# Routed expert slots: rows turned by DMA transposes of 16-bit planes instead of TensorE transposes, with eight row buffers

## The reference, cut to what matters

```python
xn = (x - mean(x)) / sqrt(var(x) + 1e-5)              # rows of 512
chosen = argmax(einsum('bsh,eh->bse', xn, gate_w))    # one of 8 experts
out = x + xn + xn @ expert_w[chosen].T                # 512 x 512 each
```

## Time and profile before

| | |
|---|---|
| median of 3 runs | 1007.43 us (1007.35 to 1007.58) |
| the profiled execution | 1007.09 us |
| its span, first to last instruction | 1005.3 us |
| PE busy | 966.4 us, 96% of the span |
| DVE busy | 674.9 us, 67% |
| ACT busy | 408.1 us, 41% |
| POOL busy | 402.1 us, 40% |
| mean granted TensorE clock | 0.989 of full speed |

### The profile page before, as it was taken

One profiled execution on the slowest core, in us unless ns is written; L12 is line 12 of the kernel. 1 busy time (PEld: TensorE's weight loads), 2 busy tenths in 40 slices (PEclk: granted clock), 3 DMA queues, 4 the chain that ended last, 5 costly groups with the idle time before them and its releaser, 6 DMA issues. The chain is left out here.

```text
span 1005.3 us, 16387 instructions
## 1 busy us (share of the span) xinstructions
PE 966.4 (96%) x5009; PEld 792.6 (79%) x5010; DVE 674.9 (67%) x1655; ACT 408.1 (41%) x704; POOL 402.1 (40%) x522
## 2 busy tenths in 40 slices
PE   7999999999999999999999999999857999999995
PEld 6788888888888888888888888888646888888884
DVE  6677777777777777777777687776985444444442
ACT  5333333333333333333333332332546666666662
POOL 1041616345261634626163362615273333333332
PEclk9999999999999999999999999999979999999998
DMA  9051022121302212130221203112265555555441
GB/s 322 12 178 43 22 105 79 48 86 42 126 32 95 83 44 88 40 126 33 95 84 43 97 31 126 41 44 85 84 220 178 159 160 166 168 159 161 138 149 55
DMA packets 47324, 101.70 MB, mean 101 GB/s; under 512 B 5781, under 2 KB 6549, under 8 KB 47264
## 3 DMA queue, kind: packets, MB, share of 16 engines
q1 hardware_dynamic: 33680, 61.93, 19.1%
q0 software_dynamic: 10800, 33.70, 8.7%
q10 hardware_dynamic: 2784, 5.31, 1.6%
HBM read 64.85 MB, written 37.90 MB: 102 GB/s over the span
## 5 line engine op out<-in xcount | busy, mean ns | idle before, releaser
L412 POOL TENSOR_TENSOR y_biased<-y_biased,gate 128x512 f32<-128x512 f32 x60 | 91.3, 1521 | 144.4 <-DVE y_biased L764 144.4
L481 POOL DMA_INDIRECT out<-gate,ids x71 | 69.9, 984 | 153.9 <-DVE gate L1029 115.2
L1355 PE MATMUL y<-expert_hi,x1T_hi 128*128 x284 | 119.3, 420 | 3.9 <-DVE x1T_lo L1023 3.9
L1029 DVE TENSOR_TENSOR gate<-y,x_rows 128x512 f32<-128x512 f32 x71 | 49.1, 691 | 108.2 <-PE y L1355 108.2
L1355 PE MATMUL y<-expert_hi,x1T_lo 128*128 x284 | 112.7, 397 | 0.0
L1355 PE MATMUL y<-expert_lo,x1T_hi 128*128 x284 | 112.3, 395 | 0.0
L1065 PE MATMUL gates<-GwT_hi,xT_hi 128*128 128x512 f32 x256 | 104.8, 409 | 0.0
L1065 PE MATMUL y<-DwT_hi,xT_hi 128*128 128x512 f32 x256 | 101.9, 398 | 0.5 <-DVE gateT L696 0.5
L1066 PE MATMUL gates<-GwT_lo,xT_hi 128*128 128x512 f32 x256 | 100.8, 394 | 0.0
L1067 PE MATMUL gates<-GwT_hi,xT_lo 128*128 128x512 f32 x256 | 100.3, 392 | 0.0
L1067 PE MATMUL y<-DwT_hi,xT_lo 128*128 128x512 f32 x256 | 100.3, 392 | 0.0
(11 more groups left out here) (246 smaller groups left out, 2372.8 us busy)
## 6 DMA issues: line engine op xcount, KB each, us to landing
x_rows<-routed_rows SPq DMA_DIRECT2D x71, 258.0 KB, 2.6
x_in<-L_attn_x SPq DMA_DIRECT2D x32, 512.0 KB, 4.4
x_rows<-L_attn_x SPq DMA_DIRECT2D x32, 512.0 KB, 4.4
raw_weights<-L_ffn_expert_w ACTq DMA_DIRECT2D x5, 1024.0 KB, 7.3
raw_weights<-L_ffn_expert_w SPq DMA_DIRECT2D x3, 1024.0 KB, 8.9
routed_rows<-padrow SPq DMA_DIRECT2D x9, 258.0 KB
out<-gate,ids POOLq DMA_INDIRECT x71, 2.8
raw_weights<-L_attn_D_w SPq DMA_DIRECT2D x1, 1024.0 KB, 8.1
```

Of the source, the lines that this page charges most:

```text
L412: nc.gpsimd.tensor_tensor(yb[:, i, :], yb[:, i, :], gate[:, i, :], ALU.mult).then_inc(S_["gated"], 1)
L481: nc.gpsimd.indirect_dma_start(out=out_rows, out_offset=bass.IndirectOffsetOnAxis(ap=ids[m][:, 0:1], axis=0), in_=res[m], in_offset=None, ...
L1029: nc.vector.tensor_tensor(res[m], Y[m % 2][:], rows[m][:, 0:D], ALU.add).then_inc(S_["slot_result"], 1)
L1355: ins = nc.tensor.matmul(Y[m % 2][:], x2T[a][:, k, m % 2 * P:(m % 2 + 1) * P], flat[w][:, bass.ds(first + k * D, D)], start=(k == 0 and a ...
```

## The change

`slot_turn` is gone from TensorE. In its place:

1. VectorE splits the normalised row of float32 into two planes of 16-bit halves: all first halves, then all second halves (`slot_split`), 1024 elements of 16 bits a partition.
2. SP issues one DMA transpose of this 128 x 1024 tile of 16-bit elements into another tile of SBUF (`flip`). It takes space in raw_weights that the expert matrices no longer need.
3. VectorE joins the planes again into float32 (`slot_merge`), into a single SBUF tile, `merged`. `slot_hi` and `slot_lo` read that tile where they read a PSUM bank before.

There are two buffers each for the halves and the turned planes, and one each for `rnorm` and `merged` (before, `rnorm` had four). The row buffers become eight (`M`), with R = 4 result buffers. The DVE order becomes merge(s + 1), sum(s - 1), lo(s + 1), split(s + 3), and ACT's hi(s + 1), norm(s + 3), base(s + 3). SP issues `load_slot(n)` and then `flip(n - 4)`. The wait for the last scattered rows, ahead of the loop of slots 48 and up before, now stands ahead of the load of slot 4, so ahead of the first flip as well.

```diff
-    M = 4
+    M, R = 8, 4
@@
-        rows = [xrow[0][:, m, :] for m in range(M)]
-        rnorm = [yb[:, m, :] for m in range(M)]
-        res = [gate[:, m, :] for m in range(M)]
+        rows = [xrow[m // NT][:, m % NT, :] for m in range(M)]
+        res = [gate[:, r, :] for r in range(R)]
+        rnorm, merged = yb[:, 0, :], yb[:, NT - 1, :]
+        halves = [yb[:, 1 + q, :].bitcast(u16) for q in range(2)]
+        flipped = [raw[:, 2, q, :].bitcast(u16).rearrange("p (k t) -> p k t", t=P) for q in range(2)]
@@ sync
+            def flip(s, q):
+
+                counted_waits(sp, (S_["slot_halves"], s + 1), (S_["slot_merged"], s - 1))
+                sp.dma_start_transpose(flipped[q], halves[q]).then_inc(slot_flip[q], 16)
+
+            AHEAD = 4
+            for m in range(AHEAD):
                 load_slot(m, m)
...
+            sp.wait_ge(rows_sent[1], 16 * NT * (NBLK // 2))
+            for m in range(AHEAD, M):
+                load_slot(m, m)
+                flip(m - AHEAD, m % 2)
             with sp.Fori(1, EARLY) as u:
                 for m in range(M):
                     load_slot(u * M + m, m)
-
-            sp.wait_ge(rows_sent[1], 16 * NT * (NBLK // 2))
+                    flip(u * M + m - AHEAD, m % 2)
@@ scalar
             def slot_hi(s, q):
-                act.wait_ge(S_["slot_turned"], s + 1)
+                act.wait_ge(S_["slot_merged"], s + 1)
                 wait(act, S_["slot_psum"], s - 1)
-                nc.scalar.activation(x2T[0][:, :, q * P:(q + 1) * P], by_block((TP, SC)[q]), ACT.Copy).then_inc(S_["slot_hi"], 1)
+                nc.scalar.activation(x2T[0][:, :, q * P:(q + 1) * P], by_block(merged), ACT.Copy).then_inc(S_["slot_hi"], 1)
...
-                wait(act, S_["slot_turned"], s - M + 1)
-                nc.scalar.activation(rnorm[m], rows[m][:, 0:D], ACT.Identity, bias=rows[m][:, SHIFT:SHIFT + 1],
+                wait(act, S_["slot_halves"], s)
+                nc.scalar.activation(rnorm, rows[m][:, 0:D], ACT.Identity, bias=rows[m][:, SHIFT:SHIFT + 1],
...
             def slot(s, m, turn):
 
-                slot_hi(s, m % 2)
-                if not (isinstance(s, int) and s == SLOTS - 1):
-                    slot_norm(s + 1, (m + 1) % M, turn + (m + 1) // M)
-                    slot_base(s + 1, (m + 1) % M)
+                if not (isinstance(s, int) and s + 1 >= SLOTS):
+                    slot_hi(s + 1, (m + 1) % 2)
+                if not (isinstance(s, int) and s + 3 >= SLOTS):
+                    enter(s + 3, (m + 3) % M, turn + (m + 3) // M)
@@ vector
+            def slot_split(s, q, pair):
+
+                dve.wait_ge(S_["slot_norm"], s + 1)
+                wait(dve, slot_flip[q], 16 * pair)
+                nc.vector.tensor_copy(halves[q].rearrange("p (h d) -> p h d", h=2),
+                                      rnorm.bitcast(u16).rearrange("p (d h) -> p h d", h=2)).then_inc(S_["slot_halves"], 1)
+
+            def slot_merge(s, q, pair):
+                counted_waits(dve, (slot_flip[q], 16 * (pair + 1)), (S_["slot_lo"], s))
+                nc.vector.tensor_copy(merged.bitcast(u16).rearrange("p (t h) -> p h t", h=2),
+                                      flipped[q].rearrange("p (h k) t -> p h (k t)", h=2)).then_inc(S_["slot_merged"], 1)
+
             def slot_lo(s, q):
                 dve.wait_ge(S_["slot_hi"], s + 1)
                 hi, lo = [h[:, :, q * P:(q + 1) * P] for h in x2T]
-                nc.vector.tensor_tensor(lo, by_block((TP, SC)[q]), hi.bitcast(f32), ALU.subtract).then_inc(S_["slot_lo"], 1)
+                nc.vector.tensor_tensor(lo, by_block(merged), hi.bitcast(f32), ALU.subtract).then_inc(S_["slot_lo"], 1)
...
             def slot(s, m, turn):
 
-                slot_lo(s, m % 2)
+                last = s if isinstance(s, int) else 0
+                if last + 1 < SLOTS:
+                    slot_merge(s + 1, (m + 1) % 2, turn * (M // 2) + (m + 1) // 2)
                 if not (isinstance(s, int) and s == 0):
                     slot_sum(s - 1, (m - 1) % M, turn - (m == 0))
+                if last + 1 < SLOTS:
+                    slot_lo(s + 1, (m + 1) % 2)
+                if last + 3 < SLOTS:
+                    slot_split(s + 3, (m + 3) % 2, turn * (M // 2) + (m + 3) // 2)
@@ tensor
-            def slot_turn(s, m):
-                bank = (TP, SC)[m % 2]
-                pe.wait_ge(S_["slot_norm"], s + 1)
-                wait(pe, S_["slot_lo"], s - 1)
-                for k in range(KD):
-                    ins = nc.tensor.transpose(bank[:, k * P:(k + 1) * P], rnorm[m][:, k * P:(k + 1) * P], ident[:])
-                ins.then_inc(S_["slot_turned"], 1)
```

More of the change, by code:

```diff
@@ L7, in preln_ssm_moe_kernel @@
                          gate_w, expert_w, out):
-    f32, f32r, bf16, i32 = mybir.dt.float32, mybir.dt.float32r, mybir.dt.bfloat16, mybir.dt.int32
+    f32, f32r, bf16 = mybir.dt.float32, mybir.dt.float32r, mybir.dt.bfloat16
+    i32, u16 = mybir.dt.int32, mybir.dt.uint16
     ALU, ACT, AX = mybir.AluOpType, mybir.ActivationFunctionType, mybir.AxisListType
@@ L112, in preln_ssm_moe_kernel @@
         dest = [kb(f"dest{q}", [P, NT], i32) for q in range(2)]
-        ids = [kb(f"ids{m}", [P, 1], i32) for m in range(M)]
+        ids = [kb(f"ids{r}", [P, 1], i32) for r in range(R)]
         count, tiles_f, cum, gap = kb("list_count", [1, E]), kb("list_tiles", [1, E]), kb("tiles_upto", [1, E]), kb("list_gap", [1, E])
@@ L178, in preln_ssm_moe_kernel @@
         row_loaded = [sem(f"row_loaded{m}") for m in range(M)]
-        out_sent = [sem(f"out_sent{m}") for m in range(M)]
+        out_sent = [sem(f"out_sent{r}") for r in range(R)]
+        slot_flip = [sem("slot_flip_even"), sem("slot_flip_odd")]
         def counted_waits(eng, *waits):
@@ L189, in by_block @@
         def by_block(bank):
-            return bank[:].rearrange("p (k t) -> p k t", k=KD)
+            return (bank if isinstance(bank, bass.AP) else bank[:]).rearrange("p (k t) -> p k t", k=KD)
         def state_tile(h, i):
@@ L365, in _ @@
                     load_slot(u * M + m, m)
+                    flip(u * M + m - AHEAD, m % 2)
             for s in range(FULL * M, SLOTS):
                 load_slot(s, s % M)
+                flip(s - AHEAD, s % 2)
+            for s in range(SLOTS - AHEAD, SLOTS):
+                flip(s, s % 2)
         @block.gpsimd
@@ L488, in slot @@
                 if not (isinstance(s, int) and s == 0):
-                    slot_store(s - 1, (m - 1) % M)
+                    slot_store(s - 1, (m - 1) % R)
             for m in range(M):
@@ L497, in _ @@
                 slot(s, s % M, FULL)
-            slot_store(SLOTS - 1, (SLOTS - 1) % M)
-            for m in range(M):
-                pool.wait_ge(out_sent[m], 16 * len(range(m, SLOTS, M)))
+            slot_store(SLOTS - 1, (SLOTS - 1) % R)
+            for r in range(R):
+                pool.wait_ge(out_sent[r], 16 * len(range(r, SLOTS, R)))
         @block.scalar
@@ L642, in slot_base, with enter @@
                                      scale=rows[m][:, GAIN:GAIN + 1]).then_inc(S_["slot_base"], 1)
+            def enter(s, m, turn):
+                slot_norm(s, m, turn)
+                slot_base(s, m)
             def slot(s, m, turn):
-                slot_hi(s, m % 2)
-                if not (isinstance(s, int) and s == SLOTS - 1):
-                    slot_norm(s + 1, (m + 1) % M, turn + (m + 1) // M)
-                    slot_base(s + 1, (m + 1) % M)
-            slot_norm(0, 0, 0)
-            slot_base(0, 0)
-            slot(0, 0, 0)
+                if not (isinstance(s, int) and s + 1 >= SLOTS):
+                    slot_hi(s + 1, (m + 1) % 2)
+                if not (isinstance(s, int) and s + 3 >= SLOTS):
+                    enter(s + 3, (m + 3) % M, turn + (m + 3) // M)
+            enter(0, 0, 0)
             experts(E_STEPS[5], NE)
-            for s in range(1, M):
+            enter(1, 1, 0)
+            enter(2, 2, 0)
+            slot_hi(0, 0)
+            for s in range(M):
                 slot(s, s, 0)
@@ L1052, in _ @@
                     slot_rows(FIRST, SLOTS - FIRST)
-            with dve.Fori(2, FULL) as u:
+            with dve.Fori(1, FULL) as u:
                 for m in range(M):
@@ L1357, in slot_product @@
                 ins.then_inc(S_["slot_psum"], 1)
-            def slot(s, m):
-                slot_turn(s, m)
-                if not (isinstance(s, int) and s == 0):
-                    slot_product(s - 1, (m - 1) % M)
             pe.wait_ge(S_["run_ready"], NBLK)
-            slot(0, 0)
             experts(E_STEPS[5], NE)
-            slot_turn(1, 1)
             pe.wait_ge(S_["expert_lo"], dve_count(NE))
@@ L1371, in _ @@
             pe.wait_ge(S_["expert_table"], 1)
-            slot_product(0, 0)
-            for m in range(2, M):
-                slot(m, m)
+            for s in range(M):
+                slot_product(s, s)
             with pe.Fori(1, EARLY) as u:
                 for m in range(M):
-                    slot(u * M + m, m)
```

(6 more changed lines are left out.)

29 lines of the change are left out of this document (17 added, 12 removed).

## The result

Four runs of the changed kernel gave a median of 1041.51 us (1040.9 to 1045.59), four of the kernel before 1007.5 on the same chip. The ratio is 1.0344, with a 95% interval from 1.0317 to 1.0372: 34 us slower, and 4.5 us above the 1037 us that were forecast.

A forecast was written before the change was run, and what follows sets the result against it. TensorE, busy 96% of the span, was taken to bound the kernel; after the change, full DMA engines at 3.6 us a slot. A 5.9 us later start plus 70 periods less 227.6 gave +30 on 1007.1: 1037 us, range 988 to 1190.

The forecast's parts named there:

- 70 P - 221.7: Change in total time: start 5.9 us later plus 70 slot periods, less 227.6 us; +30 us forecast.
- P: Slot period, from one TensorE product's start to the next: 3.6 us forecast; no change in time at 3.17.
- The copies: VectorE's split and merge, 1024 16-bit elements each: 0.70 us apiece, from the nearest float32 copies within SBUF.
- The rival of one element a cycle: VectorE's split and merge copies take 1.23 us each, period 4.0 us, 1065 us in all; chance 0.09.
- The ring D: Cycle of merge, hi, norm and split across VectorE and ScalarE, each releasing the next: 2.93 us a slot.
- The transpose's work: Time one DMA transpose takes of the 16 DMA engines: 1024 pieces at 31 ns, 2.0 us.
- The other end: Upper bound for the transpose: each of 1024 pieces costs a load packet's 0.109 us, 7.0 us of the engines.
- like the load: Rival: transposes take 0.98 us of the engines and land in 2.6; period 2.93 us, 990 us; chance 0.20.
- (D + L) / 2: Slot period set by latency, as a transpose has one iteration between split and merge: 3.4 us forecast.
- full engines: DMA engines' work a slot: load 0.98, store 0.63, transpose 2.0, together 3.6 us, taken as the period.
- L: Latency from the end of VectorE's split to the DMA transpose's turned data: 3.8 us forecast.
- The clock: Rival: TensorE idles 0.8 us a slot and drops to 1.2 GHz; period 5.1 us, 1142 us; chance 0.09.

The follow-up runs named there:

- kernel 4: Small separate program: DMA transposes, copies and loads one at a time, each awaited, plus VectorE's two 16-bit copies; a 128 x 1024 transpose lands after 3.1 us.
- Kernels 1 and 2: Changed kernel with four buffers of halves and planes, split at s + 4: 1004.91 us; changed kernel with a plain 256 KB copy replacing the transpose: 1005.24 us.
- Kernel 1: Changed kernel with four buffers each for halves and turned planes, split one slot further ahead (s + 4): 1004.91 us, ratio 0.9973.
- Kernel 7: Changed kernel with the eight padding tiles sent from GpSimd instead of SP: 1046.38 us, ratio 1.0372.
- kernel 8: Kernel before the change with only eight row buffers and the moved wait for stored rows: 1008.39 us, ratio 1.0011.
- kernel 3: Changed kernel with SP reading the next load's row number ahead of the transpose instead of behind it: 1037.28 us.
- kernel 10: Changed kernel with four buffers, row number read ahead, two buffers for normalized rows and ScalarE five slots ahead: 1010.19 us, ratio 1.0027.
- kernel 12: Kernel before with odd slots from 7 on turned by DMA transpose, split five slots ahead, the others by TensorE: 994.79 us, ratio 0.987.
- kernel 9: Changed kernel with four buffers of halves and planes and SP's row number read ahead of the transpose: 1016.31 us, ratio 1.0072.

## Why the prediction held, and where its reason was off

- **The direction and the sum.** The formula was 70 P - 221.7. With the measured P of 3.65 it gives 1007.1 + 33.9 = 1041.0; the profiled execution took 1041.1. So all of the miss of that execution, 4 us, is in P, 3.65 for 3.6.
- **The copies**, taken at 0.70 from a float32 row: 0.73 and 0.77 us in the slots (split and merge). In kernel 4, with nothing beside them, they take 0.69 and 0.74. The rival of one element a cycle, 1.23 us, falls.
- **The ring D**, 2.93: measured 2.91 on the mean. Kernels 1 and 2 show it bare, 2.98 from merge to merge in the median.
- **The transpose's work**, 2.0 us of the engines from the row nearest in piece size (31 ns a packet): 1.6 us in the slots by the estimate above, 25 ns a packet, and 1.3 us alone. The other end, 109 ns a packet, falls, and so does "like the load" (0.98).
- **What sets P: here the reason was off.** The prediction had (D + L) / 2 = 3.4 from latency and 3.6 from full engines, and took the larger. The engines' work is 3.3, and they were 0.90 busy, so they did not set P. It was the latency: from 2 x 3.65 - 2.91, L = 4.4 us and not 3.8, and the 49 merges that a transpose held up show the same, 4.5 us behind the split. The term mis-sized is the landing. It was added up from the load's 2.6 us, taken with the engines half idle. That the load and the store beside it make it longer fits the 3.1 us that a transpose takes alone, but no run took just these two away. Kernel 1 decides between the theories: same transposes, one more iteration of slack, 37 us back.
- **Luck in the number.** Two errors met. With the measured 1.6 us for the transpose in place of 2.0, the prediction's own sum gives the engines 3.2 us and the latency (2.93 + 3.4) / 2 = 3.2 us, so P = 3.2 and 1010 us, close to no change. The 2.0 us, too much for the engines' work, stood in for the longer landing. The size of the forecast loss rests on that luck. The ring, the slack and the rule for P are what was understood.
- **The two rules that pointed apart.** The Trainium skill, page "VectorE: DVE Perf Modes" (The three transpose paths), gives 1309 ns for one 128 x 128 block on the DMA path; eight in series would be an estimated 10.5 us. The trace of kernel 4 does not agree with adding them up: eight blocks in one instruction land in 3.1 us. The Trainium skill, page "DMA: Bandwidth & Descriptors" (Latency and other measured facts), gives an effective 261 GB/s, an estimate of 1.0 us for this tile. The traces do not agree with that either: the transpose takes the engines 1.3 us alone and 1.6 us in the slots.
- **The start**, 770.4 forecast, 770.3 measured. Kernel 7 shows that moving the padding tiles away wins nothing.
- **Eight row buffers**, put at nothing: 1.1 us at the start, in kernel 8.
- **The clock** stayed at 1.00 from 775 us to the last product, with waits of up to 1.6 us between products, so this rival did not come true. Other kernels here came closer: in kernel 3 one wait of 1.77 us was followed by a granted clock of 0.55 (872 to 874 us), and in kernel 10 the waits of 3.00 and 3.68 us by one of 0.50.

## What to carry to other kernels

A step moved from a compute engine to a DMA brings latency: count iterations of slack between its start and its use, and let the slack cover the landing beside the other traffic, not the landing alone. Here one iteration more of slack was worth 37 us and no instruction less. Then balance: TensorE relieved of all transposes only moved the limit to the ring and the DMA side (its engines or its queue on SP), at 1004.9 us. Relieved of half of them (kernel 12) the kernel took 994.8 us, less than with none or all.

## What the runs showed that was not expected

- The instruction right behind a DMA transpose on its queue can be held: a register read takes 0.79 us instead of 0.27 with nothing else running (kernel 4), a load's issue 1.0 instead of 0.34 (kernel 9), though not in kernel 3, where it is 0.35 in the median.
- Transposes among padding stores land after up to 15.3 us, and hold SP for up to 5.2 (kernel 7).
- Where VectorE's merge meets GpSimd's copy of the row numbers, both are longer. In kernel 1, from 800 to 985 us, they meet at 52 merges of 60. There the merge takes 0.89 us on the mean for 0.75 and the copy 0.60 for 0.19:

```profile
864.38 0.91 DVE L1056 COPY y_biased<-raw_weights 128x1024 uint16<-128x1024 uint16 x1
864.73 0.60 POOL L497 COPY ids<-x_rows 128x1 int32<-128x1 int32 x1
```
